# A tuned transformer kernel on one core: the second attention takes q and k as plain float32, with its two kinds of score products on the two halves of the array

## The reference

```
y        = layernorm(x) * norm_w + norm_b, features cut to 256 >> e in block e
q, k, v  = y @ (q_w, k_w, v_w) + biases            # features of head h
P        = softmax(q k^T / sqrt(256))              # over all 2048 positions
out      = P v,   then out_proj, residual, layernorm
```

## Time and profile before

| | us |
|---|---|
| median of three runs | 5153.57 (5153.51 to 5154.35) |
| span of the profiled execution, first to last instruction | 5142.3 |
| what the median has beyond the span | 11.3 |
| stage `at2`, from its first maxima to its last sums | 4170 to 5030 |

### The profile page before, as it was taken

One profiled execution on the slowest core, in us unless ns is written; L12 is line 12 of the kernel. 1 busy time (PEld: TensorE's weight loads), 2 busy tenths in 40 slices (PEclk: granted clock), 3 DMA queues, 4 the chain that ended last, 5 costly groups with the idle time before them and its releaser, 6 DMA issues. The chain is left out here.

```text
span 5142.3 us, 90411 instructions
## 1 busy us (share of the span) xinstructions
PE 4714.6 (92%) x34043; PEld 2092.5 (41%) x34043; DVE 4237.0 (82%) x5517; ACT 3449.7 (67%) x6176; POOL 1333.4 (26%) x881
## 2 busy tenths in 40 slices
PE   6999786797999999999999999999998879999993
PEld 3444452364333333333333333333334445555542
DVE  6999650397899999999999999999993877777736
ACT  4787310132688888888888888888886326666663
POOL 2233220164000000000000000000001229999992
PEclk9999897898899999999999999999998669999996
DMA  5110479688333333343333344333322941222305
GB/s 182 52 53 33 155 247 385 251 280 232 45 53 48 48 48 48 54 54 51 48 48 48 50 54 53 50 48 48 49 34 76 313 128 42 71 70 67 78 10 167
DMA packets 390773, 498.42 MB, mean 97 GB/s; under 512 B 165440, under 2 KB 278880, under 8 KB 373312
## 3 DMA queue, kind: packets, MB, share of 16 engines
q1 hardware_dynamic: 372448, 465.90, 38.7%
q10 hardware_dynamic: 17888, 26.74, 1.5%
HBM read 325.15 MB, written 165.02 MB: 95 GB/s over the span
## 5 line engine op out<-in xcount | busy, mean ns | idle before, releaser
L792 DVE TENSOR_REDUCE at_NM<-at_MX 128x1 f32<-128x1024 f32 (+1 forms) x3008 | 3085.0, 1050 | 299.5 <-PE at_MX L614 270.9
L734 ACT ACTIVATE at_PB<-at_S 128x512 f32<-128x512 f32 x5056 | 2719.4, 597 | 585.9 <-PE at_S L643 466.0
L614 PE MATMUL at_MX<-at_KT,at_QT 48*128 48x512 f32 (+1 forms) x5056 | 1919.7, 455 | 60.2 <-DMA at_VS<-v 45.6
L643 PE MATMUL at_S<-at_QT,at_KT 50*128 50x512 f32 (+1 forms) x5056 | 1899.9, 441 | 6.0 <-ACT at_PB L734 5.8
L655 PE MATMUL at_AV<-at_PB,at_VS 128*32 128x256 f32 (+1 forms) x18304 | 1567.7, 414 | 16.7 <-ACT at_AVS L742 15.7
L643 PEld LDWEIGHTS at_S<-at_QT,at_KT 50*128 50x128 f32 (+1 forms) x5056 | 801.8, 187 | 876.6 <-ACT at_PB L734 772.0
L614 PEld LDWEIGHTS at_MX<-at_KT,at_QT 48*128 48x128 f32 (+1 forms) x5056 | 791.6, 190 | 311.0 <-DVE at_NM L792 217.7
L655 PEld LDWEIGHTS at_AV<-at_PB,at_VS 128*32 128x32 f32 x18304 | 364.6, 108 | 858.6 <-ACT at_PB L734 745.4
L548 POOL CAST at_NMR<-at_NMF 16x128 fp32r<-16x128 f32 x79 | 22.1, 280 | 1625.3 <-ACT at_NMF L747 1625.3
L575 POOL TENSOR_TENSOR at_SUM<-at_SUM,at_PB 128x2048 f32<-128x2048 f32 x90 | 415.4, 4615 | 10.9
L932 PE MATMUL wkv_PQ<-wkv_XT,wkv_WT 128*128 128x512 f32 x768 | 339.6, 600 | 42.5 <-DVE wkv_DL L1052 25.9
(11 more groups left out here) (209 smaller groups left out, 3531.4 us busy)
## 6 DMA issues: line engine op xcount, KB each, us to landing
moe_W<-in_w SPq DMA_DIRECT2D x64, 1024.0 KB, 11.9
at_QT<-qk SPq DMA_DIRECT2D x402, 128.0 KB, 5.2
at_KT<-qk SPq DMA_DIRECT2D x384, 128.0 KB, 6.6
qk<-r_HI SPq DMA_DIRECT2D x52, 512.0 KB, 5.0
qk<-r_LO SPq DMA_DIRECT2D x52, 512.0 KB, 5.3
at_VS<-v SPq DMA_DIRECT2D x96, 256.0 KB, 9.2
at_KT<-qk SPq DMA_DIRECT2D x96, 256.0 KB, 6.2
ycat<-wkv_Y SPq DMA_DIRECT2D x32, 512.0 KB, 2.6
```

The lines of the kernel that those rows point to most:

```text
L614: ins = nc.tensor.matmul(MX[r][:, a, :], q_of(s)[h:h + NQ, b * P:(b + 1) * P], k_of(it, s, b * P // W)[h:h + NQ, (c + a) * W:(c + a + 1) * W],
L643: nc.tensor.matmul(SP_[item(it, s, "score", t)[1]][:, :], k_of(it, s, c)[h:h + NQ + 2, kb * P:(kb + 1) * P], q_of(s)[h:h + NQ + 2, c * W:( ...
L734: nc.scalar.activation(PB[:, t % NPB, :], SP_[r][:, :], ACT.Exp, scale=scale).then_inc(exp_done, 1)
L792: nc.vector.tensor_reduce(NM4[:, b, c:c + 1], MX[r][:, :, :].rearrange("p a n -> p (a n)"), AX_X, ALU.max, negate=True).then_inc(ring_got, 1)
```

## The change

In `at2` (`not TWO`) q and k are held once, as float32, instead of as three stacked pairs of float32r parts. `NQ` becomes 32. Each q and k tile has two copies of the same 32 rows: at partitions 0 to 31 for the maxima and at 64 to 95 for the scores (`MAX_AT`, `SCORE_AT`). A row more goes with each: row 32 of q is zero against a row of ones in k, row 96 of q holds minus the maximum against a row of ones. Both products thus use 33 rows. GpSimd clears rows 32 to 63 of the three q tiles first, `set_ones` fills whole k tiles, and SyncE's first k loads now wait for it (`front_set`). The split of the maximum in two parts on GpSimd goes; SyncE copies ScalarE's `NMF` straight into the q tile. In `r6` the LO parts, their VectorE instructions and their stores go; HI becomes QK, float32. `at1` is as before. The words that came with the change also speak of "row sums from eight pairs", but the diff has no line on `GROUPS`, `add` or `sums`: the additions and sums stay as they are.

The diff, without the renamed semaphores, the set-up of the two zero and front waits and the lines that only follow from the rest:

```diff
@@ -271,9 +271,11 @@
     NBLK = T // P
     W = 512
     NCH = T // W
-    NQ = 3 * DH
-    TWO = NQ + 2 <= 64
-    HALVES = (0, 64) if TWO else (0,)
+    TWO = DH + 1 <= 32
+    NQ = 3 * DH if TWO else DH
+    DT = F32R if TWO else F32
+    HALVES = (0, 64)
+    SCORE_AT, MAX_AT = 64, 0
     VW = 32
     NSB = NCH * NBLK
     NPB = 36
@@ -362,17 +364,17 @@
 
     with ExitStack() as ctx:
         m = Mem(nc, ctx, tag)
-        QT = [m.sb(f"QT{u}", [P, T], F32R) for u in range(NQB)]
-        KT = [m.sb(f"KT{u}", [P, T], F32R) for u in range(NKB)]
+        QT = [m.sb(f"QT{u}", [P, T], DT) for u in range(NQB)]
+        KT = [m.sb(f"KT{u}", [P, T], DT) for u in range(NKB)]
         VS = [m.sb(f"VS{u}", [P, NBLK, VW]) for u in range(NKB)]
         PB = m.sb("PB", [P, NPB, W])
         AVS = [m.sb(f"AVS{u}", [P, W]) for u in range(2)]
         NM4 = m.sb("NM4", [P, NBLK, NMX // NBLK])
         NM = m.sb("NM", [P, NBLK])
         NMF = m.sb("NMF", [NBLK, P])
-        NMR = m.sb("NMR", [NBLK, 2, P], F32R)
         ident = m.sb("ident", [P, P])
         if TWO:
+            NMR = m.sb("NMR", [NBLK, 2, P], F32R)
             O = [m.sb(f"O{u}", [P, NBLK, DH]) for u in range(2)]
             REC = [m.sb(f"REC{u}", [P, W // P, NCH]) for u in range(2)]
             FO = [m.sb(f"FO{u}", [P, W]) for u in range(2)]
...
@@ -402,6 +404,8 @@
 
         def set_ones(eng, u):
 
+            if not TWO:
+                return eng.memset(KT[u][:, :], 1.0)
             for h in HALVES:
                 lo = (h + NQ) // 32 * 32
                 ins = eng.memset(KT[u][lo:lo + 32, :].bitcast(F32), 1.0)
...
@@ -448,9 +452,9 @@
         def load_queries(eng, it, bh, c, e, count):
 
             u = it % NQB
-            for k, part in enumerate((0, 0, 1)):
-                eng.dma_start(QT[u][k * DH:(k + 1) * DH, c * W:(c + count) * W].bitcast(F32),
-                              qk_d[0, part][bh][:, e * W:(e + count) * W]).then_inc(loaded[u], 16)
+            for h in HALVES:
+                eng.dma_start(QT[u][h:h + DH, c * W:(c + count) * W],
+                              qk_d[0][bh][:, e * W:(e + count) * W]).then_inc(loaded[u], 16)
 
         @block.sync
         def _(sp):
@@ -463,9 +467,8 @@
                         load_queries(sp, it, bh, c, e, count)
                     if bh in FRESH[it] and (bh, e) == next(lane for lane in units[it] if lane[0] == bh):
                         k_at = KSLOT[bh]
-                        for k, part in enumerate((0, 1, 0)):
-                            sp.dma_start(KT[k_at][k * DH:(k + 1) * DH, :].bitcast(F32),
-                                         qk_d[1, part][bh]).then_inc(loaded[u], 16)
+                        for h in HALVES:
+                            sp.dma_start(KT[k_at][h:h + DH, :], qk_d[1][bh]).then_inc(loaded[u], 16)
                         sp.dma_start(VS[k_at][:, :, :], v_d[bh]).then_inc(loaded[u], 16)
 
             def load(it, s):
@@ -485,6 +488,11 @@
 
             def m_row(it, s):
 
+                if not TWO:
+                    wait(sp, nmf_got, it + 1)
+                    row = SCORE_AT + NQ
+                    sp.dma_start(q_of(s)[row:row + 1, :], NMF[:, :]).then_inc(mrow, 16)
+                    return
                 wait(sp, nmr_ready, it + 1, sp_step)
                 for h in HALVES:
                     for a in range(2):
@@ -512,6 +520,7 @@
                         sp.dma_start(ident[:, :], ident_d).then_inc(const_ld, 16)
                         sp.wait_ge(loaded[0], 16 * NLOAD)
             else:
+                sp.wait_ge(front_set, 2)
                 load_lanes(0)
                 sp.dma_start(ident[:, :], ident_d).then_inc(const_ld, 16)
                 sp.wait_ge(loaded[0], loads(0, 0))
@@ -535,6 +544,10 @@
 
         @block.gpsimd
         def _(pool):
+            if not TWO:
+                for u in range(NQB):
+                    nc.gpsimd.memset(QT[u][MAX_AT + NQ:MAX_AT + NQ + 32, :], 0.0).then_inc(zero_set, 1)
+                pool.wait_ge(zero_set, NQB)
             for u in range(2, NKB):
                 set_ones(nc.gpsimd, u).then_inc(back_set, 1)
             if not TWO:
...
@@ -609,6 +623,12 @@
                     wait(pe, loaded[s % NQB], loads(it, s))
                 wait(pe, ring_got, seq - RING + 1)
                 b, c = divmod(x * MXW, T // W)
+                if not TWO:
+                    rows = slice(MAX_AT, MAX_AT + NQ + 1)
+                    nc.tensor.matmul(MX[r][:, 0, :], q_of(s)[rows, b * P:(b + 1) * P],
+                                     k_of(it, s, b * P // W)[rows, c * W:(c + 1) * W],
+                                     start=True, stop=True).then_inc(ring_put, 1)
+                    return
                 for a in range(MXW):
                     h = 64 * a
                     ins = nc.tensor.matmul(MX[r][:, a, :], q_of(s)[h:h + NQ, b * P:(b + 1) * P],
@@ -636,13 +656,16 @@
             def scores(it, s, t):
 
                 kb, c = divmod(t, NCH)
-                h = HALVES[t % len(HALVES)]
+                rows = slice(SCORE_AT, SCORE_AT + NQ + 1)
+                if TWO:
+                    h = HALVES[t % len(HALVES)]
+                    rows = slice(h, h + NQ + 2)
                 if t == 0:
-                    wait(pe, mrow, 32 * len(HALVES) * (it + 1))
+                    wait(pe, mrow, (64 if TWO else 16) * (it + 1))
                 slot_free(it, "score", t)
                 nc.tensor.matmul(SP_[item(it, s, "score", t)[1]][:, :],
-                                 k_of(it, s, c)[h:h + NQ + 2, kb * P:(kb + 1) * P],
-                                 q_of(s)[h:h + NQ + 2, c * W:(c + 1) * W], start=True, stop=True).then_inc(s_put, 1)
+                                 k_of(it, s, c)[rows, kb * P:(kb + 1) * P],
+                                 q_of(s)[rows, c * W:(c + 1) * W], start=True, stop=True).then_inc(s_put, 1)
 
             def values(it, s, kb, part):
@@ -742,7 +765,10 @@
                 nc.scalar.activation(AVS[s % 2][:, :], AV[:, :], ACT.Copy).then_inc(avs_ready, 1)
 
             def take_turned(it, i, r):
-                wait(act, nmr_ready, it)
+                if TWO:
+                    wait(act, nmr_ready, it)
+                else:
+                    wait(act, mrow, 16 * it)
                 wait(act, s_put, i + 1)
                 nc.scalar.activation(NMF[:, :], SP_[r][0:NBLK, 0:P], ACT.Copy).then_inc(nmf_got, 1)
...
@@ -1425,14 +1450,13 @@
             def store_qkv(g):
                 b, e = divmod(g, E4)
                 u = g % 2
-                qk = qk_d.rearrange("a l (b h) d t -> b a l (h d) t", b=B)[b]
+                qk = qk_d.rearrange("a (b h) d t -> b a (h d) t", b=B)[b]
                 for a in range(2):
                     cs, k = (CC, P) if a else (len(rows(e)), rows(e)[0])
-                    wait(sp, lo_done, so_far(g, CC * a + cs - 1))
-                    for part, tile in enumerate((HI, LO)):
-                        out = qk[a, part].rearrange("(c p) t -> p c t", p=P)
-                        sp.dma_start(out[0:k, 0:cs, e * GT:(e + 1) * GT],
-                                     tile[u][0:k, CC * a:CC * a + cs, :].bitcast(F32)).then_inc(l_st[u], 16)
+                    wait(sp, qk_done, so_far(g, CC * a + cs - 1))
+                    out = qk[a].rearrange("(c p) t -> p c t", p=P)
+                    sp.dma_start(out[0:k, 0:cs, e * GT:(e + 1) * GT],
+                                 QK[u][0:k, CC * a:CC * a + cs, :]).then_inc(l_st[u], 16)
                 wait(sp, v_done, g + 1)
                 out = v_d.rearrange("(b h) p n w -> b p h n w", b=B)[b]
                 sp.dma_start(out[:, :, e * J:(e + 1) * J, :], VB[u][:, :, :, :]).then_inc(l_st[u], 16)
...
@@ -1550,21 +1574,23 @@
                 wait(act, vproj, g - 1)
                 nc.scalar.activation(XT[g % 2][:, :, :], PT[:, :, :], ACT.Copy).then_inc(xt, 1)
 
-            def high(g):
+            def take_qk(g):
                 e, u = g % E4, g % 2
-                wait(act, l_st[u], 80 * (g // 2))
+                wait(act, l_st[u], 48 * (g // 2))
+                if g == 0:
+                    act.wait_ge(b_done, 2)
                 for a in range(2):
                     wait(act, proj, 2 * g + a + 1)
                     for c in range(CC if a else len(rows(e))):
                         q = a * CC + c
-                        nc.scalar.activation(HI[u][:, q, :], PO[a][:, c, :], ACT.Identity,
-                                             bias=BCE[:, e, q:q + 1]).then_inc(hi_done, 1)
+                        nc.scalar.activation(QK[u][:, q, :], PO[a][:, c, :], ACT.Identity,
+                                             bias=BCE[:, e, q:q + 1]).then_inc(qk_done, 1)
 
             act.wait_ge(const_ld, 16 * 6)
             for g in range(NGR):
                 shifted(g)
                 copy_turned(g)
-                high(g)
+                take_qk(g)
 
         @block.vector
         def _(dve):
@@ -1609,19 +1635,10 @@
```

(18 more changed lines are left out.)

19 lines of the change are left out of this document (8 added, 11 removed).

## The result

The changed kernel takes 5734.59 us (median of 4 runs, 5721.27 to 5744.39) against 5153.54 for the kernel before beside it (5146.32 to 5154.35): ratio 1.1131, interval 1.1113 to 1.1149, so 581 us slower. Forecast were 5728 us and a range of 5545 to 5850.

What follows compares the result with a forecast made beforehand. The prediction took TensorE to bound `at2`'s middle units, with POOL close behind; 94 + 345 + 25 + 110 = 574 us took the span from 5142.3 to 5716, with 11.3 more 5728 us; range 5545 to 5850.

Steps and rivals of the forecast that it cites:

- The price of a float32 product: On TensorE: two records of 0.43 us, so 0.86 us a product against 0.233 for float32r.
- Full overlap of a pair: In `at2`: maxima and scores on two row halves overlap fully, 0.86 us for a pair; 1.72 without overlap.
- the rival of the kept order: In `at2`: scores' first record starts beside the maxima's second, +94 us and some 10 more, 5830 us; chance 0.20.
- Term 2: 86 maxima tiles ahead of unit 0: TensorE alone decides at 1.2 GHz, 147 us instead of 53, +94 us.
- Term 3: First unit of `at2`: starts at 1.2 GHz, about 50 us at half clock, +25 us (between 0 and +60).
- Term 4: Scores alone, 86 steps in units 13 and 14: +42 us at 2.4 GHz, +141 at 1.2, taken as +110.
- my two thirds of the way: Scores alone in units 13 and 14: point chosen between +42 us (2.4 GHz) and +141 (1.2 GHz), giving +110.
- The rival of a clock at 2.4 GHz: Clock stays at 2.4 GHz wherever TensorE has no pause: +408 us, 5562 us; chance 0.15.
- The zeros: `r6`, and loads, memsets and maximum's transfer in `at2`: no change, 0 us, the start of `at2` within 5 either way.
- The 11.3 us: Added to the forecast span of 5716 us, as the median of the runs lies that far beyond the profiled span.
- The rival on the other side: In `at2`: a 33-row float32 product costs only 0.233 us, period 2.1 us, GpSimd decides, 5125 us; chance 0.02.
- term 1: Periods with maxima in `at2`: 4.63 us against 3.05, +25.3 us a unit, 13.66 units, +345 us.

Runs made afterwards that it cites:

- Experiments 5 and 6: Changed kernel with q and k as one float32r high part, 33 rows and then 64 rows: 5169.83 us (ratio 1.0037) and 5139.81 us (0.9975).
- experiment 2: Changed kernel with maxima and scores both on the lower half of the rows, so that they cannot overlap: 8033.04 us (one run).
- Experiment 1: Changed kernel with zero rows of q added, so both products take 64 rows of their half instead of 33: 5620.36 us, ratio 1.0912.
- experiment 7: Changed kernel with 64 rows for each product, tiles ahead and last 86 scores alternating between the halves: 5523.01 us, ratio 1.0720.
- experiment 4: Kernel before without LO instructions and stores in `r6`; `at2` loads HI in place of LO, scale divided by three: 5150.72 us, ratio 1.0001.
- experiment 3: Changed kernel with the 86 maxima tiles ahead put by turns on both halves, 33 rows each: 5677.99 us, ratio 1.1024.
- experiment 10: Changed kernel with row sums over eight groups of two key blocks instead of five groups: 5749.11 us, ratio 1.1148.

## Why the prediction was right, point by point

**The price of a float32 product, right.** It was 2 records of 0.43; the period came out at 4.63 as worked out, units 1 to 12 grew by 25.2 us each against 25.3. Experiments 5 and 6 turn it round: take the second record away and leave the rest, and the time is within 0.4% of before. So the second record is what costs, for all that these runs can tell apart.

**Full overlap of a pair, right, and the rival of the kept order wrong.** The pairs start together and the period has no record more than eight. By the Trainium skill (TensorE: Matmul & The Clock Gate, Part 3) matmuls start and end strictly in program order. Taken for every record, as the forecast took it, the period would be 5.06; the trace does not agree, at 4.63, with the scores' first record beside the maxima's first. Taken for whole products the trace agrees: the maxima product starts and ends first, by 0.01 us or less. That overlap is there at all, experiment 2 shows by taking it away.

**Terms 2 to 4, right in mechanism, the sizes near.** Term 2 measured 93.8 on TensorE and 96.8 to the first exponential (94): the tiles stayed at 1.2 GHz. Term 3 was 25 for a slow first unit and measured 56.9 - 25.2 = 31.7: the clock rose 68 us into it, not after about 50, with the first group of sums behind values. Term 4 was 110 and measured 137.8 - 42/64 x 25.2 = 121: my two thirds of the way were four fifths. The two thirds were a choice between 42 and 141, not worked out. The rival of a clock at 2.4 GHz fell on the same rows. The Trainium skill (the same page, Part 1) has it that sustained activity releases the throttle; here PE was busy 149.35 of 151 us and then 68 of 68 at 0.50, and the trace does not agree if activity is read as time without pause. Experiment 1 shows what is missing: rows. Zero rows, with not one product more, gave back 114 us. No run is the rival's case: experiment 1 has 5620 with the tiles ahead still at half clock, and experiment 7, which has 1.00 nearly everywhere, also puts the tiles and the last scores two at a time.

**The zeros, right.** `r6`: 197.0 both times, and experiment 4 at 1.0001. The start: 19.9 us against 20.9. But what it waits for is another thing than I named. The chain ahead of the first maxima tile (timeline, kernel after):

```profile
4165.12 5.28 POOL L549 MEMSET at_QT<- 32x2048 f32 x3 [22.47 <-POOLq L90]
4170.46 8.78 POOL L408 MEMSET at_KT<- 128x2048 f32 x5
4179.30 0.12 POOL L555 MEMSET at_ONES<- 128x32 f32 x1
4179.52 2.90 PE L628 MATMUL at_MX<-at_KT,at_QT 33*128 33x512 f32 x3 [19.97 <-POOL at_ONES L555]
```

The 14 us of memsets on GpSimd are now last; the loads with fewer bytes are ready before them. It came out even by chance, and a memset more would have shown: in experiment 1 GpSimd waits 5.71 us for three more on VectorE, and the same gap is 25.6 us. The last of the first loads had landed at 4178.2, 1.1 us before GpSimd was through.

**What was off, and evened out.** The 11.3 us that the forecast added behind the span do not lie behind it: this execution has 1.8 there. In all executions listed the time is 1.7 to 3.0 us beyond the span, so most of the 11.3 was a quick profiled execution of the kernel before against its median. Terms 2 to 4 were together 20 too small (2.8 + 6.7 + 11). And the profiled execution after is itself 10 above its median, with 10.1 us more in phases that the change does not touch: some 6 are in `at1`, where the clock rose at 1350.7 instead of 1333.7. The forecast came within 7 us of the median, while its terms missed the 594 us of the tiles ahead and the units by 20: the nearness of the one is in part luck. The rival on the other side has a slip in words: a pair at one record would make a period three tenths shorter, not a pair a quarter of a period; its 2.1 us is right.

**What stays open.** Why pairs of 33 rows with values between them held 1.00 in the middle units while pairs alone (experiment 3) did not raise it, and pairs with values did so only once sums stood beside the values: the runs show it, they don't explain it. Experiment 2's 2300 us are lost overlap and lost clock together. By its expectation the overlap alone is worth about 750; that is an estimate, no run separates the two. Experiment 7 minus before is 373 us, of which 345 are term 1, in middle units of 78.6 us that no float32 layout tried here made shorter.

## What to carry to other kernels

Before changing a matmul's type, count the records that it leaves and the spacing between them in a trace: here three stacked parts in one float32r record (0.233 us) cost a quarter of the two float32 records (0.86 us) that replaced them, and halves of the array that overlap win back only a factor of two. Look at the granted clock of stretches in which few rows are in use, however busy PE is; where it is low, try zero rows up to the edge of the half: they did not lengthen a product and were worth 114 us here, 5.7 us of longer start included. And work removed from an engine that waits anyway (35 us of VectorE in `r6`, GpSimd's additions while TensorE is the bound) is worth nothing until the bound has moved.

## What the runs showed of the hardware that was not expected

- Zero rows change the granted clock. With the same products, waits and product lengths, 64 rows instead of 33 turned 94.8 + 144.1 us of units 13 and 14 into 78.5 + 77.4, at 1.00 where it had been 0.52 from 5443 us on.
- PE without a pause over 3470 us was granted 0.53 (experiment 2), with 33 or 34 rows on one half and values of 128 rows between them.
- With float32 products of 33 rows the clock came back only next to sums of 128 rows behind values: 2.8 us after the first group started in the change, 3.1 in experiment 3, 1.1 in experiment 10.
- Two float32 products on the two row halves interleave record by record, at full clock 0.01 us apart at most, and cost no more together than one alone (4.63 us a period against 4.62).
- A float32 product of 512 columns takes the same 0.86 us with 33 and with 64 rows (units of 78.58 us both times).
